# Expert matmuls of a routed feed-forward layer with the weights as the stationary side, in plain float32 on copied weights

## The reference

```
h = _layernorm(x) * (1 + cb) + sb
gate_logits = einsum('bsd,de->bse', h, gate_kernel)          # 8 experts, the best 2 of each token
combine = softmax of the two best logits, at their experts
h0 = einsum('bsd,edm->bsem', h, w0_kernel)                   # 256 -> 512
h1 = einsum('bsd,edm->bsem', h, w1_kernel)                   # 256 -> 512
inter = silu(h0) * h1
out = einsum('bse,bsem,emd->bsd', combine, inter, wo_kernel) # 512 -> 256
x = x + gb * out
```

## Time and profile before

| | us |
|---|---|
| time, median of 2 runs | 409.71 (408.59 to 410.83) |
| the profiled execution's own time | 410.27 |
| its span in the trace | 408.4 |
| PE busy | 366.0 |
| DVE busy | 261.6 |
| POOL busy | 226.9 |
| ACT busy | 168.6 |

### The profile page before, as it was taken

The page is one execution under the profiler, slowest core; times in us unless marked ns, Lnnn a source line. Parts: engine busy times, 40 slices in busy tenths (PEclk is TensorE's granted clock), DMA queues, the critical chain, the costliest instruction groups (busy, mean ns, idle before and its releaser), DMA issues.

```text
span 408.4 us, 11445 instructions
## 1 busy us (share of the span) xinstructions
PE 366.0 (90%) x3888; PEld 270.9 (66%) x3889; DVE 261.6 (64%) x723; ACT 168.6 (41%) x258; POOL 226.9 (56%) x172
## 2 busy tenths in 40 slices
PE   1995899999989959899998899999999999999980
PEld 1763547666666746566664588888888888888860
DVE  4285645767764786765674477777777777777740
ACT  2250444546254404124222255555555555555520
POOL 3021161544763475264466277777777777777751
PEclk9996889999998988889999999999999999999996
DMA  6946028019903960549569434333433433333322
GB/s 243 263 129 246 3 92 268 20 30 344 287 10 85 323 242 6 153 155 201 95 197 319 88 78 80 78 78 78 78 78 78 77 60 82 61 80 70 52 26 26
DMA packets 35390, 50.62 MB, mean 124 GB/s; under 512 B 4996, under 2 KB 22296, under 8 KB 35352
## 3 DMA queue, kind: packets, MB, share of 16 engines
q1 hardware_dynamic: 25112, 36.17, 31.2%
q0 software_dynamic: 8176, 13.65, 14.9%
q10 hardware_dynamic: 2064, 0.28, 0.6%
HBM read 31.93 MB, written 18.16 MB: 123 GB/s over the span
## 4 chain that ended last, share of the span: by engine, by line
PE 77%; issue 5%; DMA 5%; DVE 4%; ACT 4%; SPq 3%; POOL 1%; POOLq 0%; ACTq 0%; DVEq 0%
PE ps L1677 15%; PE ps L1392 8%; PE ps L1657 7%; PE ps L1658 7%; PE ps L1661 7%; PE ps L1648 5%; PE ps L1669 4%; PE ps L1511 3%; PE ps L1419 3%; PE ps L1400 3%; PE ps L1485 3%; PE ps L1453 2%; PE ps L1579 2%; PE ps L1529 2%; DMA out_dram<-wg_s,qd 2%
## 5 line engine op out<-in xcount | busy, mean ns | idle before, releaser
L635 POOL TENSOR_TENSOR w_lo<-we,w_hi 128x1024 fp32r<-128x1024 f32 x30 | 74.2, 2472 | 25.1 <-ACT w_hi L824 25.1
L1677 PE MATMUL ps<-we,qeo 128*128 x312 | 75.6, 385 | 1.4 <-ACT qeo L809 0.8
L1677 PEld LDWEIGHTS ps<-we,qeo 128*128 128x128 f32 x312 | 57.2, 189 | 18.1 <-issue 10.5
L809 ACT COPY qeo<-ps 128x512 f32<-128x512 f32 x39 | 22.9, 586 | 106.9 <-PE ps L1669 106.9
L645 POOL DMA_INDIRECT out_dram<-wg_s,qd x30 | 46.7, 1556 | 25.3 <-issue 12.9
L1298 DVE TENSOR_TENSOR w_halves<-we,w_halves 128x1024 fp32r<-128x1024 f32 x30 | 36.8, 1225 | 7.2 <-ACT w_halves L824 7.2
L1648 PE MATMUL ps<-we,xn 128*128 x72 | 35.5, 617 | 0.4 <-issue 0.4
L1270 DVE CAST rT_halves<-ps 128x256 fp32r<-128x256 f32 x30 | 12.7, 425 | 33.5 <-PE ps L1579 33.5
L824 ACT CAST w_hi<-we 128x1024 fp32r x30 | 31.6, 1053 | 0.0
L824 ACT CAST w_halves<-we 128x1024 fp32r x30 | 31.4, 1048 | 0.0
L1657 PE MATMUL ps<-w_halves,rT_halves 128*128 128x512 f32 x60 | 29.2, 487 | 0.0
(11 more groups left out here) (235 smaller groups left out, 728.5 us busy)
## 6 DMA issues: line engine op xcount, KB each, us to landing
rowbuf<-routed SPq DMA_DIRECT2D x39, 260.5 KB, 2.9
we<-in_ffn_w_kernel_dram SPq DMA_DIRECT2D x16, 512.0 KB, 5.7
we<-in_ffn_wo_kernel_dram SPq DMA_DIRECT2D x8, 512.0 KB, 6.9
routed<-z SPq DMA_DIRECT2D x9, 260.5 KB, 3.6
xrows<-in_attn_x_dram SPq DMA_DIRECT2D x4, 512.0 KB, 13.8
out_dram<-xrows SPq DMA_DIRECT2D x4, 512.0 KB, 4.2
we<-in_wmod_dram SPq DMA_DIRECT2D x1, 1536.0 KB, 7.2
sbcb<-gsc_dram SPq DMA_DIRECT2D x4, 256.0 KB, 4.5
```

The lines of the kernel that those rows point to most:

```text
L635: g.tensor_tensor(w_lo[1], expert_up(e, 1), w_hi[1].bitcast(F32), ALU.subtract)\
L1677: last = mm(down_ps, eit[s % 2][:, k, :], weights(e, 2 * FT * F + k * D, D), start=k == 0, stop=k == KF - 1)
```

## The change

All 39 tiles now have one form. ACT copies the expert's w0 and w1 as they are, in float32, to `w_whole`, of which there are two sets by turns (`weights_whole`), also for the early tiles. `up` takes a 128x128 block of these copies as the stationary side and the turned rows, 128 columns, as the moving side: 4 blocks of the inner width by 2 blocks of features by 2 weights, 16 float32 products of 128 columns. The result has the inner width on partitions and tokens on columns, which is what the outer product needs, so `hidden` writes `eit` directly, and the transposes of `turn_hidden`, the copy of `turn_back` and the `it_full` and `it_act` semaphores go. The high and low parts, on ACT, DVE and POOL, go. The copies for tile 0 stand on ACT before `group_normed` of the last batch, behind waits for the table, the expert weights and the last values of the attention.

```diff
-        rT_halves = half("rT_halves", [P, 2, 2, FT, P], "xn", 0)
-        w0_halves = half("w0_halves", [P, 2, FT * F], "vx", 0)
-        w1_hi, w1_lo = half("w1_hi", [P, FT * F], "parts", 0), half("w1_lo", [P, FT * F], "kT", 0)
+        w_whole = [[nc.alloc_sbuf_tensor_at(f"w{u}{v}", [P, FT * F], F32, offset=offset[n] + 4 * o)[:, :]
+                    for v, (n, o) in enumerate(places)]
+                   for u, places in enumerate(((("vx", FT * F), ("kT", 0)), (("vx", 0), ("parts", 0))))]
...
-            def weights_lo(i, s):
-                e = pool.value_load(table(i)[0:1, 1, bass.ds(i, 1)], min_val=0, max_val=E - 1)
-                pool.wait_ge(w_hi_ready[1], i + (1 - EARLY))
-                g.tensor_tensor(w_lo[1], expert_up(e, 1), w_hi[1].bitcast(F32), ALU.subtract)\
-                    .then_inc(w_lo_ready[1], 1)
...
-            def turn_back(i, s):
-                act.wait_ge(it_full, i + 3)
-                act.wait_ge(dn_full, i + 1)
-                a.copy(eit[s % 2], ps[5][:, :].rearrange("p (k n) -> p k n", k=KF)).then_inc(it_act, 1)
...
+            def weights_whole(i, s, which):
+                const = isinstance(i, int)
+                if const and i == EARLY and which == 0:
+                    act.wait_ge(tab_ready, 4)
+                if const and i == 0 and which == 0:
+                    act.wait_ge(tab_ready, 2)
                     act.wait_ge(we_in, 16 * 3 * E)
+                    act.wait_ge(pv_done, SETS * B)
                 e = act.value_load(table(i)[0:1, 1, bass.ds(i, 1)], min_val=0, max_val=E - 1)
+                if not (const and i < 2):
+                    settle(act, [((up0_full, up1_full)[which], i + (-1))], act_passed)
+                a.copy(w_whole[s % 2][which], expert_up(e, which)).then_inc(whole_ready[which], 1)
...
             def hidden(i, s):
                 dve.wait_ge(up1_full, i + 1)
                 dve.wait_ge(in_done, 2 * i + 5)
-                dve.wait_ge(it_full, i + 1)
-                v.tensor_tensor(ein[s % 2], eth[s % 2], up_ps[s % 2][1][:, :], ALU.mult).then_inc(in_done, 1)
+                dve.wait_ge(dn_full, i + 1)
+                v.tensor_tensor(eit[s % 2].rearrange("p k n -> p (k n)"), eth[s % 2], up_ps[s % 2][1][:, :],
+                                ALU.mult).then_inc(in_done, 1)
...
-            def weights_lo(i, s):
-                e = dve.value_load(table(i)[0:1, 1, bass.ds(i, 1)], min_val=0, max_val=E - 1)
-                dve.wait_ge(w_hi_ready[0], i + (1 - EARLY))
-                v.tensor_tensor(w_lo[0], expert_up(e, 0), w_hi[0].bitcast(F32), ALU.subtract)\
-                    .then_inc(w_lo_ready[0], 1)
...
+            def up(i, s, which, done):
+                pe.wait_ge(whole_ready[which], i + 1)
+                for f in range(KF):
+                    for k in range(FT):
+                        last = mm(up_ps[s % 2][which][:, f * P:(f + 1) * P],
+                                  w_whole[s % 2][which][:, k * F + f * P:k * F + (f + 1) * P], rT[s % 2][:, k, :],
+                                  start=k == 0, stop=k == FT - 1)
                 last.then_inc(done, 1)
...
-            def turn_hidden(i, s):
-                pe.wait_ge(in_done, 2 * i + 6)
-                pe.wait_ge(it_act, i + 1)
-                for k in range(KF):
-                    last = tr(ps[5][:, k * P:(k + 1) * P], ein[s % 2][:, k * P:(k + 1) * P], ident[:, :])
-                last.then_inc(it_full, 1)
```

More of the change, by code:

```diff
@@ L647, in add_rows @@
                     compute_op=ALU.add).then_inc(added, 16)
-                if not (isinstance(i, int) and not EARLY <= i + 3 < N_TILES):
-                    weights_lo(i + 3, s + 3)
             pool.wait_ge(x2_out, 16 * (B - 1))
@@ L832, in act_step @@
                     tanh_part(i, s)
-                if not (isinstance(i, int) and not EARLY <= i + 1 < N_TILES):
+                if not (isinstance(i, int) and i + 1 >= N_TILES):
                     for which in range(2):
-                        weights_hi(i + 1, s + 1, which)
+                        weights_whole(i + 1, s + 1, which)
+            for which in range(2):
+                weights_whole(0, 0, which)
             group_normed(b)
@@ L1266, in take_rows @@
                 turned = ps[4][:, 0:D].rearrange("p (k n) -> p k n", k=FT)
[L1267 to L1272 removed]
+                v.tensor_copy(rT[s % 2], turned).then_inc(rt_dve, 1)
                 dve.wait_ge(added_ok, i + 1)
@@ L1312, in dve_step @@
                     silu_mul(i, s)
-                if not (const and not EARLY <= i + 1 < N_TILES):
-                    weights_lo(i + 1, s + 1)
             b = B - 1
@@ L1692, in pe_step @@
                 if here:
-                    if early(i):
-                        e = pe.value_load(table(i)[0:1, 1, bass.ds(i, 1)], min_val=0, max_val=E - 1)
                     pe.wait_ge(rt_dve, i + 1)
                     pe.wait_ge(in_done, 2 * i + 2)
-                    upward(i, s, e, 0, up0_full)
+                    up(i, s, 0, up0_full)
                 if between is not None:
                     between()
-                if before:
-                    turn_hidden(i - 1, s - 1)
                 if not (const and i + 1 >= N_TILES):
@@ L1706, in pe_step @@
                 if here:
[L1707 removed]
+                    up(i, s, 1, up1_full)
                 if before_down is not None:
```

54 lines of the change are left out of this document (5 added, 49 removed).

## The result

The changed kernel took 422.65 us, median of two runs (420.40 and 424.91), against 409.71 of the kernel before. The medians stand at 1.032; the ratio reported with the result is 1.038 (95% interval 1.027 to 1.048). The forecast was 414.7. Three later sets of runs, on other occasions and each beside the kernel before, gave less. All 20 runs of the changed kernel have a mean of 417.8 us, 82 runs of the kernel before a mean of 409.9. The change costs 7.9 us (plus or minus 1.9), a ratio of 1.019 (1.015 to 1.024). The ratios reported with a set of runs leave out as slow those more than 1.5% above the fastest run of their kernel, while all other figures here take every run.

A forecast was written before the change was run, and what follows sets the result against it. PE was taken to bound the late tiles; 408.4 - 0.5 - 0.1 + 6.5 + 0.2 - 1.1 = 413.4 us of span, 415.3 with 1.87 outside, 414.7 after the profiled run's 0.56 above median; range 409 to 423.

The forecast's parts named there:

- The late tile: PE, tiles 9 to 37: 32 products at 0.1115 us make 5.52 us a tile against 5.29, +6.5 us over 28 tiles.
- The parts of the old tile: Old late tile on PE: inner products 3.04 us, transposes 0.43 + 0.14, outer product 1.73, summed as 5.2.
- the 7.0 case: Rival, late tiles on PE: weight loads not hidden, 32 pairs at 0.219 us take 7.0; about 545 us, chance 0.03.
- The expert's number is read in time: Against the rival of a late register read before the outer product: some 0.5 us a tile, 430 us; all such gaps 0.26.
- ACT's copies: Late tiles: two copies of 1.05 us, hidden with 0.6 us to spare; rival that they set the tile, counted within gaps' 0.26.
- The queue for instructions: Rival, PE in the late loop: larger body must be fetched, 2.9 us in each of seven passes; +20, 435 us, chance 0.03.
- -0.5 us up to tile 8's rows: Early stages: DVE reaches the ranks about 0.5 us earlier, so tile 8's load comes 0.5 us earlier.
- -0.1 from there to tile 9: PE from 226.05 to 235.40: the new order takes 9.29 us against 9.35, or -0.1.
- 0.2 for the longer way: Added in the sum as +0.2 us for the last late tile, beside the +6.5 for 28 tiles.
- The push by the copies: First tile: ACT's copies push the last group norm from 173.65 to about 174.3 and PE by 0.7 to 0.9 us.
- The end: From tile 36's outer product on: 5.2 + 0.85 + 4.58 + 7.65 = 18.3 us against 19.4, -1.1.
- The sum: Whole kernel: 408.4 - 0.5 - 0.1 + 6.5 + 0.2 - 1.1 = 413.4 us of span, giving a forecast of 414.7 us.

The follow-up runs named there:

- a_64_columns: Changed kernel with inner products streaming only the first 64 of a tile's 128 rows, weight loads unchanged: median 421.4 us, +10.0 (±3.1) to the kernel before.
- b_longer_wait: Kernel before with one more padding write behind a wait for the others' landing, so tile 8's rows come later: median 413.5 us, +2.7 (±3.4).
- a_late_only: Changed kernel with the old form kept in the first nine tiles, new form in the other 30: median 417.9 us, +7.1 (±3.2) to the kernel before.
- b_no_pool_low: Kernel before without POOL's low part of w1 and the wait for it, PE using the high part twice: mean -2.6 us (±1.8).

## Why the prediction was right or wrong

**The late tile: right to the hundredth.** Forecast 5.52 us with a distance of 0.1115; measured 5.518 and 0.112. The 28 tiles came to +6.4 us against +6.5. All it rested on were the router's products with 8 columns, and a_64_columns confirms the reason given: the load is the longer one and hides the stream. The granted clock was 1.00 and PE had no gap. The trace did hold a nearer pair than the prediction says: each float32 transpose has its own 128x128 load ahead of 128 columns, and they follow at 0.109 us. In the kernel before, from 200 us on:

```profile
L1669 PEld LDWEIGHTS ps<-ident,sm 128*128 128x128 f32 x144 | 17.7, 141 | 5.7 <-DVE sm L1285 0.9 <-issue 0.8
```

Two sums of the prediction are off without touching the forecast. The parts of the old tile (3.04, 0.57, 1.73) come to 5.34 and not to 5.2, more than a whole tile, since the 3.04 has waits in it. And "the 7.0 case" is the inner products alone; the tile would have been 9.

**The rivals about the late tile fall.** The expert's number is read in time, even with 16 short pairs ahead of it; there is no issue time ahead of the outer product. ACT's copies take 1.043 us as in the earlier trace rows, and no late product waited for one. The queue for instructions fetched 2 packets from 236 to 385 us where the earlier trace rows had 1, and PE was busy throughout, so no pass of the loop waited for code. POOL waits for DVE's weighting, 87.3 us in 22 waits between 236 and 400 us, and sets nothing.

**The start of the last batch and the early tiles: here it failed.** The prediction counted -0.5 us up to tile 8's rows, -0.1 from there to tile 9, and 0.2 for the longer way from a tile's first matmul to the outer product: -0.4 up to the outer product of tile 8. In the table this comes at 69.3 us on average of the four traces of the changed kernel. The eight traces with the old form in the first tiles, b_longer_wait left out, have 68.1: +1.1 (±1.7). The push by the copies was forecast rightly: the first inner product starts 0.9 us later on average (forecast 0.7 to 0.9), with a wait of 1.51 us for the copy in three traces and 0.49 in the fourth. What the sum lacked was a term for the clock: it compared counts at the clock of the one profile, and named the clock as a danger only for the late tiles, where it was right that nothing happens. The changed kernel spent 6.0 us at half clock from the zero up to 235 us on average, the kernels with the old form 2.6. The difference of 3.4 us at half speed is worth some 1.7 us by my estimate, 0.7 of it ahead of tile 8's rows and 1.1 behind. Without it -0.5 and -0.1 are left, which is the forecast.

How much of this the change causes is not shown. The +1.1 is within its own error, and a_late_only, whose first nine tiles are the old form, takes 244.5 us from the zero to the end, as the changed kernel does on average (244.6).

**The end: half right.** Forecast -1.1; the traces show -0.5 on average (20.8 against 21.4 in the table). POOL's low parts no longer hold an add, as b_no_pool_low shows in the old kernel. The term that was too small is the way from the outer product to the add. The end of the changed kernel on PE, DVE and POOL:

```profile
397.78 1.89 PE L1629 MATMUL ps<-we,qeo 128*128 x8
...
399.81 0.48 DVE L1268 SCALAR_TENSOR_TENSOR wg_s<-ps,qd 128x256 f32<-128x256 f32 x1 [1.15 <-PE ps L1629]
...
401.10 1.54 POOL L633 DMA_INDIRECT out_dram<-wg_s,qd  x1 [3.96 <-DVE wg_s L1268]
406.40 1.54 POOL L633 DMA_INDIRECT out_dram<-wg_s,qd  x1 [3.77 <-DVE wg_s L1268]
411.01 1.54 POOL L633 DMA_INDIRECT out_dram<-wg_s,qd  x1 [3.07 <-DMA out_dram<-wg_s,qd]
```

Tile 36's outer product ends at 399.67 and its add starts at 401.10: 1.43 us where the sum took 0.85. The add of tile 37 comes one tile later, the last one 4.61 us after it, as in the earlier trace rows.

**The sum.** From the traces the change makes +1.1 (up to tile 8) + 6.4 - 0.5 (the end) = 7.0 us, against -0.4 + 6.5 - 1.1 = 5.0 forecast; the runs say 7.9 (±1.9). The step that failed is the one from the profile's sum to the time. It put the clock in the stages before the late tiles at nothing, where the traces show half clock worth some 1.7 us more in the changed kernel; and it took one start of the kernel as given. The gain at the end was also forecast 0.6 us too large. The first result was 12.9 us, 5.0 above the mean difference of all runs; its profiled execution lost 5.4 us ahead of anything that the change touches. That part is the luck of two runs and no error of the mechanism. A profile and two runs of kernels whose single runs spread by 16 us could not tell these apart. The late tile, from which the prediction got its sign, was right. Whether the clock falls more readily behind the new form's steps, and why, stays open.

## What to carry to other kernels

Read a weight load's price from a product with hardly any columns to stream, and compare it with the stream: at 128 columns of float32 the two are about equal here (0.112 us, and 0.108 estimated for the stream), and at 64 and 8 columns the load set the distance. A wait on a semaphore ahead of a register read shows up as "issue" far from its cause, and moving the read in among queued matmuls took 0.14 us off each of 28 tiles here (5.29 to 5.15). When a stretch before the one you cost has idle time, give the clock a term of its own in the sum, and ask for more than one trace of the kernel before.

## What the runs showed of the hardware

- Executions of the same code differ by 8 us in when the clock rises to its upper level at the start (16 to 17 us or 25 us); the same matmuls then came 4.3 us later. By 45 us two of the seven traces with a late rise had made it up, having no stretch at half clock in between.
- In a stretch that was otherwise at full clock, a single wait of 4.74 us for rows brought 6.8 us at half clock (b_longer_wait, one trace). Waits of 2.1 to 2.8 us did so in four of nine traces.
- Loads of 128 x 128 float32 weights that use all rows overlap the matmul before them: 0.112 us a pair with 128 columns and with 64.
- A register read on PE's sequencer behind a semaphore wait showed as 0.2 to 0.6 us of issue in 16 places, 0.14 us a tile on average (5.29 to 5.15).
